# Transposes of an attention kernel on 32-row tiles, four at a time, into the score banks

## The chip, the core and the metric
The kernel runs on one core of one Trainium2 chip. The metric is the device time of one execution in microseconds (us). Before the change it was 661.67 us, the median of 3 runs (661.62 to 662.46). The core has five engines with queues of their own: TensorE (PE; the profile shows its weight loads as PEld), VectorE (DVE), ScalarE (ACT), GpSimd (POOL) and SyncE (SP, which only issues DMAs here).

## The reference
Attention with 12 heads of 32 channels over 64 batch elements of 128 tokens and 384 channels, then a residual and a normalisation without weights. Both encodings are `adj`, so the bias is twice `adj`.

```python
scale = 384 ** (-0.5)
q = (x @ Wq.T).reshape(b, n, 12, 32)
k = (x @ Wk.T).reshape(b, n, 12, 32)
v = (x @ Wv.T + bv).reshape(b, n, 12, 32)
bias = (adj + adj)[:, None]
scores = einsum('bqhd,bkhd->bhqk', q, k) * scale + bias
row_nonzero = any(scores != 0, axis=-1, keepdims=True)
scores = where(row_nonzero, scores, -inf)
p = nan_to_num(softmax(scores, axis=-1))
out = einsum('bhqk,bkhd->bqhd', p, v).reshape(b, n, h)
x = layernorm(x + (out @ Wo.T + bo))
```

## The kernel before
Everything is float32. The four weight products are each made of three matmuls in the rounded form fp32r (high by high, high by low, low by high: `TERMS`), so x, the weights and the attention output are split into a high part (a copy to fp32r on ACT) and a low part (a subtraction on POOL or DVE).

Batch elements are worked on one by one, in an order written out by hand for each engine. Keys and queries are projected for a group of four batch elements together (`GRP`): six tiles (`TILES`) of 128 channels by 512 tokens, three of keys and three of queries, nine matmuls each (`project`, L279). `projected(b)` (L153) deals these six tiles to four iterations as 2, 1, 2, 1, one group ahead of their use. Iteration b then does the following on PE (L375 to L398): scores of b+1 (`score`, L296: per head one product of 32 channels, so the array is used as four tiles of 32 rows, and head j of each four goes to bank `scores_ps[j]`), the transposes of the softmax numerators of b in three turns of four heads (`turn`, L325), the values of b+1 (`values`, L311), the projections in between, the output projection of b-1 (`project_out`, L357), the transposes of the normalising factors (`turn_scale`, L332) and the product of numerators and values (`attend`, L342: 128 rows, 32 columns of weights).

All transposes write one PSUM bank, `pt_ps`, which is emptied each time: four heads by ACT (L466), twice four by DVE (`keep_turned`, L511), the factors by ACT (L481). One bank, `qk_ps`, takes the projections of keys and queries, one, `vo_ps`, both the values and the output projection, and one, `att_ps`, the attention. Four are the score banks.

DVE (L571 to L587) reads the scores, adds the bias and finds the row maxima (`bias_and_max`, L498), adds the value bias (`keep_v`, L507), finds the factors (`find_scale`, L518 to L526), multiplies the attention by them (`normalise`, L534), makes its low part (`attention_low`, L538) and the residual with its statistics (`residual`, L547 to L552). ACT (L459 to L484) has the exponentials with row sums (L409, four heads in `softmax_top`), the copies of projected tiles (`keep`, L420), the high parts of the attention (L431) and of x (`split_x_high`, L426) and the end of the normalisation (L439). POOL (L250 to L258) has the tree that adds up scores to see whether a row is zero (`sum_scores`, L230), the output bias (L219), the inverse deviation (L238 to L244) and the low part of x (`split_x_low`, L212). The split of x for group g runs two groups ahead, in iterations with b % 4 of 0, 1 and 2; the first tile of a group waits for all of it at L273.

Of the kernel before, what the change touches and what calls it, by code (L numbers as in the profile page):

```python
# [10 lines left out]
P = 128  # L11
# [15 lines left out]
TERMS = ((HI, HI), (HI, LO), (LO, HI))  # L27
TREE = 3
# [4 lines left out]
def build(nc, xt, xn, adj, wq, wk, wv, wo, bv, bo, out):  # L33
    with ExitStack() as ctx:
# [27 lines left out]
        probs_t = sb("probs_t", [P, HEADS, P])  # L62
# [5 lines left out]
        scale_t = sb("scale_t", [P, HID])  # L68
# [24 lines left out]
        first_ps = [*scores_ps, qk_ps, vo_ps]  # L93
# [28 lines left out]
        pt_first = sem("pt_first")  # L122
        pt_rest = sem("pt_rest")
# [6 lines left out]
        scale_turned = sem("scale_turned")  # L130
        scale_t_ready = sem("scale_t_ready")
# [71 lines left out]
        def _(pool):  # L203
# [46 lines left out]
            for b in range(-1, NB + 2):  # L250
                if has(b - 2):
                    find_rstd(b - 2)
                if has(b):
                    add_bias(b)
                if has(b + 1):
                    sum_scores(b + 1)
                if 0 <= b and b % GRP < KT and b // GRP + 2 < NG:
                    split_x_low(b // GRP + 2, b % GRP)  # L258

        @block.tensor  # L260
        def _(pe):
            def run_idle(count):

                for _ in range(count):
                    nc.tensor.matmul(pt_ps[:].rearrange("p j q -> p (j q)"), zeros[:, 0:P], zeros[:], start=True,  # L265
                                     stop=True)

            def project(tile):
# [3 lines left out]
                if t == 0:  # L272
                    pe.wait_ge(x_split, KT * g)  # L273
                if tile == 0:
                    pe.wait_ge(first_keys, KT)
                wait(pe, kept, tile)
                for k in range(KT):
                    for n, (a, c) in enumerate(TERMS):
                        last = nc.tensor.matmul(qk_ps[:], w[:, a, k, cols], x_t[:, g % XBUFS, c, k],  # L279
                                                start=(k == 0 and n == 0),  # L280
                                                stop=(k == KT - 1 and n == len(TERMS) - 1))
                last.then_inc(proj_done, 1)
# [45 lines left out]
            def turn_scale(b):  # L328
                pe.wait_ge(scale_ready, b + 1)
                pe.wait_ge(pt_rest, 2 * b + 2)  # L330
                for m in range(KT):
                    last = nc.tensor.transpose(pt_ps[:, m], scale_n[:, b % 2, m * P:(m + 1) * P], ident[:])  # L332
                last.then_inc(scale_turned, 1)

            def attend(b):

# [38 lines left out]
            for b in range(-1, NB + 1):  # L375
                tiles = projected(b)
                if has(b + 1):
                    score(b + 1)
                if has(b):
                    turn(b, 0)  # L380
                if len(tiles) == 2:
                    project(tiles[0])
                if has(b + 1):
                    values(b + 1)
                if has(b):
                    turn(b, 1)
                if tiles:
                    project(tiles[-1])
                if has(b):
                    turn(b, 2)  # L390
                if has(b - 1):
                    project_out(b - 1)
                if has(b):
                    turn_scale(b)
                    attend(b)
                if b == NB - 1:
                    pe.wait_ge(scale_t_ready, NB)
# [3 lines left out]
        def _(act):  # L401
            def softmax_top(b, m):
                act.wait_ge(biased, KT * b + m + 1)
                if m == 0:
                    wait(act, turned, KT * (b - 1))
# [8 lines left out]
            def keep(tile):  # L414
# [5 lines left out]
                nc.scalar.activation(dst[:, g % 2, t % KT], qk_ps[:], ACT.Copy, scale=scale).then_inc(kept, 1)  # L420

            def split_x_high(g, k):
# [3 lines left out]
                nc.scalar.activation(x_t[:, g % XBUFS, HI, k], x_raw[:, g % 2, k], ACT.Copy).then_inc(x_high, 1)  # L426

# [31 lines left out]
            for b in range(-1, NB + 2):  # L459
                tiles = projected(b)  # L460
                if has(b - 1):
                    attention_high(b - 1)
                if has(b):
                    act.wait_ge(turned, KT * b + 1)
                    wait(act, pv_done, b)
                    nc.scalar.activation(probs_t[:, 0:HPT], pt_ps[:], ACT.Copy).then_inc(pt_first, 1)  # L466
                if has(b + 1):
                    softmax_top(b + 1, 0)
                if len(tiles) == 2:
                    keep(tiles[0])  # L470
                if has(b + 1):
                    softmax_top(b + 1, 1)
                    softmax_top(b + 1, 2)
                if tiles:
                    keep(tiles[-1])
                if has(b - 2):
                    normalised(b - 2)
                if has(b):
                    act.wait_ge(scale_turned, b + 1)
# [143 lines left out]
```

## Time and profile before

| | |
|---|---|
| median of 3 runs | 661.67 us |
| the profiled execution | 661.33 us |
| its span, first to last instruction | 659.5 us |
| granted TensorE clock | 0.999 of full speed |
| PE, ACT, DVE, POOL busy | 638.3, 517.6, 502.6, 410.4 us |
| HBM traffic | 68 GB/s over the span |

The span is the profiled execution less some 1.8 us around it. A busy PE is not PE at its peak: matmuls overlap and their ends are modelled, so the distance from one start to the next tells more than one record's duration. Idle time of the other engines costs nothing as long as PE does not wait for them.

### The profile page before, as it was taken

The page shows a single profiled execution, that of the slowest core. Times are in us where ns is not written, and L with a number is a line of the kernel's source. Part 1 is how long each engine was busy: PE and PEld are TensorE (multiplying, and loading weights), DVE is VectorE, ACT ScalarE, POOL GpSimd, SP SyncE. Part 2 cuts the span into 40 slices and gives each one's busy share as a digit, 9 for nine tenths or more (in the row PEclk, how much of TensorE's full clock was granted, in tenths as well). Part 3 has the DMA queues.
Part 4 walks back from the last instruction along what each step waited for, and adds up shares of the span by engine and source line. Part 5 has one row for each costly group of instructions (what it writes and reads, how often), then busy time and mean ns, then how long its engine had stood idle before and what let it go on. Part 6 is the DMA issues. An engine that isn't in the chain of part 4 may idle for free.

```text
span 659.5 us, 18322 instructions
## 1 busy us (share of the span) xinstructions
PE 638.3 (97%) x6060; PEld 550.3 (83%) x6060; DVE 502.6 (76%) x2319; ACT 517.6 (78%) x1942; POOL 410.4 (62%) x500
## 2 busy tenths in 40 slices
PE   9999999999999999999999999999999999999774
PEld 5788888888888888888888888888888888888673
DVE  4667887877887777887877887777877877877884
ACT  5678887878878788877878878788877878877782
POOL 1557665756756666765766856666765756845662
PEclk9999999999999999999999999999999999999999
DMA  9300312121121210212121131210212111011111
GB/s 306 122 4 9 106 57 105 57 74 44 48 105 58 104 50 19 95 59 104 58 86 41 38 106 58 104 50 29 85 58 105 57 50 36 32 58 58 49 49 49
DMA packets 17951, 45.88 MB, mean 70 GB/s; under 512 B 1984, under 2 KB 7104, under 8 KB 17856
## 3 DMA queue, kind: packets, MB, share of 16 engines
q1 hardware_dynamic: 17424, 44.11, 19.3%
q8 instruction: 49, 0.80, 0.5%
q10 hardware_dynamic: 432, 0.59, 0.3%
q14 instruction: 46, 0.38, 0.2%
HBM read 32.11 MB, written 12.58 MB: 68 GB/s over the span
## 4 chain that ended last, share of the span: by engine, by line
PE 67%; POOL 16%; issue 8%; DVE 7%; ACT 2%; POOLq 0%
PE qk_ps L279 21%; PE vo_ps L357 11%; POOL tree L230 10%; PE vo_ps L311 10%; PE pt_ps L325 9%; PE scores_ps L296 6%; PE att_ps L342 5%; DVE nscores L498 4%; POOL x_t L212 4%; PE pt_ps L332 2%; ACT probs L409 2%; PE scores_ps L369 1%; PE pt_ps L265 1%; POOL x_n L219 1%; DVE att_t L538 1%
## 5 line engine op out<-in xcount | busy, mean ns | idle before, releaser
L409 ACT ACTIVATE probs<-nscores,neg_max 128x128 f32<-128x128 f32 x768 | 296.7, 391 | 3.1 <-DVE neg_max L498 3.1
L498 DVE CUSTOM_DVE_ANT_0 nscores<-scores_ps,adj_n 128x128 f32<-128x128 f32 x768 | 171.6, 286 | 16.0 <-PE scores_ps L296 16.0
L409 ACT ACTIVATION_READ_ACCUMULATOR probs<-nscores,neg_max 128x1 f32 x768 | 146.5, 191 | 0.0
L230 POOL TENSOR_TENSOR tree<-nscores 128x768 f32<-128x768 f32 x64 | 120.2, 1878 | 36.0 <-DVE neg_max L498 36.0
L325 PE MATMUL pt_ps<-ident,probs 128*128 128x128 f32 x768 | 118.7, 277 | 9.2 <-ACT probs L409 7.0
L357 PE MATMUL vo_ps<-w_o,att_t 128*128 128x384 f32 x576 | 116.8, 347 | 0.0
L212 POOL TENSOR_TENSOR x_t<-x_raw,x_t 128x512 fp32r<-128x512 f32 x45 | 58.4, 1300 | 93.5 <-ACT x_t L426 93.5
L311 PE MATMUL vo_ps<-w_v,x_t 128*128 128x384 f32 x576 | 114.1, 342 | 0.0
L325 PEld LDWEIGHTS pt_ps<-ident,probs 128*128 128x128 f32 x768 | 89.8, 140 | 28.9 <-ACT probs L409 7.9
L230 POOL TENSOR_TENSOR tree<-tree 128x384 f32<-128x384 f32 (+1 forms) x128 | 103.8, 811 | 10.0
L279 PE MATMUL qk_ps<-x_t,w_k 128*128 128x512 f32 x405 | 105.4, 404 | 2.6 <-POOL x_t L212 2.6
L279 PE MATMUL qk_ps<-x_t,w_q 128*128 128x512 f32 x405 | 105.3, 404 | 0.0
L511 DVE COPY probs_t<-pt_ps 128x512 f32<-128x512 f32 x128 | 87.4, 683 | 19.9 <-PE pt_ps L325 19.9
L311 PEld LDWEIGHTS vo_ps<-w_v,x_t 128*128 128x128 f32 x576 | 100.0, 188 | 2.8
L357 PEld LDWEIGHTS vo_ps<-w_o,att_t 128*128 128x128 f32 x576 | 97.9, 189 | 0.8 <-DVE att_t L538 0.8
L279 PEld LDWEIGHTS qk_ps<-x_t,w_k 128*128 128x128 f32 x405 | 72.7, 188 | 20.1 <-POOL x_t L212 6.0
L279 PEld LDWEIGHTS qk_ps<-x_t,w_q 128*128 128x128 f32 x405 | 72.7, 188 | 14.1
L547 DVE TENSOR_TENSOR y<-vo_ps,x_n 128x384 f32<-128x384 f32 x64 | 35.7, 557 | 53.5 <-PE vo_ps L357 53.5
L219 POOL TENSOR_TENSOR x_n<-x_n,bo_rows 128x384 f32<-128x384 f32 x64 | 65.1, 1017 | 17.4 <-DMA x_n<-xn 17.4
L431 ACT ACTIVATE att_t<-att_ps 128x384 fp32r<-128x384 f32 x64 | 31.4, 491 | 45.3 <-DVE att_ps L534 45.3
L507 DVE TENSOR_TENSOR v_n<-vo_ps,bv_rows 128x384 f32<-128x384 f32 x64 | 35.5, 555 | 40.6 <-PE vo_ps L311 40.6
L481 ACT ACTIVATE scale_t<-pt_ps 128x384 f32<-128x384 f32 x64 | 31.4, 491 | 44.5 <-PE pt_ps L332 43.2
(56 smaller groups left out, 808.2 us busy)
## 6 DMA issues: line engine op xcount, KB each, us to landing
x_n<-xn SPq DMA_DIRECT2D x32, 384.0 KB, 3.6
out<-out_n SPq DMA_DIRECT2D x32, 384.0 KB, 2.6
x_raw<-xt SPq DMA_DIRECT2D x15, 768.0 KB, 5.4
adj_n<-adj SPq DMA_DIRECT2D x32, 128.0 KB, 2.0
x_raw<-xt SPq DMA_DIRECT2D x3, 256.0 KB, 5.5
nscores<-wq ACTq DMA_DIRECT2D x3, 192.0 KB, 4.2
nscores<-wk SPq DMA_DIRECT2D x3, 192.0 KB, 5.5
probs<-wv SPq DMA_DIRECT2D x1, 576.0 KB, 6.4
```

The costliest lines, as they stand in the source:

```text
L212: nc.gpsimd.tensor_tensor(x_t[:, g % XBUFS, LO, k], x_raw[:, g % 2, k], x_t[:, g % XBUFS, HI, k].bitcast(F32), ALU.subtract).then_inc(x_sp ...
L219: nc.gpsimd.tensor_tensor(row, row, bo_rows[:], ALU.add).then_inc(xb_ready, 1)
L230: nc.gpsimd.tensor_tensor(tree[:, b % 2, :, 0:width], src[:, :, 0:width], src[:, :, width:2 * width], ALU.add).then_inc(tree_step, 1)
L279: last = nc.tensor.matmul(qk_ps[:], w[:, a, k, cols], x_t[:, g % XBUFS, c, k], start=(k == 0 and n == 0), stop=(k == KT - 1 and n == len(T ...
L296: last = nc.tensor.matmul(scores_ps[j][:, m * P:(m + 1) * P], q_t[rows, g % 2, m, cols], k_t[rows, g % 2, m, cols], start=True, stop=True)
L311: last = nc.tensor.matmul(vo_ps[:, 0:HID], x_t[:, g % XBUFS, a, k, cols], w_v[:, c, k], start=(k == 0 and n == 0), stop=(k == KT - 1 and n ...
L325: last = nc.tensor.transpose(pt_ps[:, j], probs[:, b % 2, m * HPT + j], ident[:])
L357: last = nc.tensor.matmul(vo_ps[:, 0:HID], att_t[:, a, k], w_o[:, c, k], start=(k == 0 and n == 0), stop=(k == KT - 1 and n == len(TERMS) ...
L409: last = nc.scalar.activation(probs[:, b % 2, h], nscores[:, b % 2, h], ACT.Exp, bias=neg_max[:, b % 2, h:h + 1], scale=-1.0, accum_out=ro ...
L498: last = nc.vector.tensor_tensor_reduce(out=nscores[:, half, h], in0=scores_ps[j][:, m * P:(m + 1) * P], in1=adj_n[:, b // 2 % 2, half], s ...
L511: nc.vector.tensor_copy(probs_t[:, m * HPT:(m + 1) * HPT], pt_ps[:]).then_inc(pt_rest, 1)
L547: nc.vector.tensor_tensor(y[:, half], vo_ps[:, 0:HID], x_n[:, b // 2 % 2, half], ALU.add).then_inc(y_ready, 1)
```

## The change
- The numerators are transposed in pieces of 32 tokens. `turn` takes, for each head, four transposes of 32 rows by 128 keys with a 32x32 piece of the identity, one on each row tile, into the four score banks; then, after a wait for `scale_ready`, the three tiles of factors in the same manner. That is 48 + 12 transposes in place of 12 + 3, in one stretch, after the scores in these banks have been read (`biased`). Each bank ends up with 15 x 32 columns.
- `probs_t` grows by three tiles and takes numerators and factors together (`scale_t` goes). ACT copies two of the banks (`keep_turned_low`), DVE two (`keep_turned_high`); `attend` and `normalise` wait for both.
- `pt_ps` goes, and `qk_ps` gets a second bank, used by turns. The six tiles of a group are dealt as 2, 1, 2, 1, with one before the values and, where there are two, the second after the turn.
- On ACT the first eight heads come before the copies, the last four after; on DVE all heads' biases come first, then `find_scale`, `attention_low`, `keep_v`, the copies and `residual`.
- x is split one iteration sooner (`split_in`), and the first projection waits for its parts one at a time.

```diff
-        qk_ps = ps("qk_ps", [P, 512])
+        qk_ps = [ps(f"qk_ps{i}", [P, 512]) for i in range(2)]
-        pt_ps = ps("pt_ps", [P, HPT, P])
 
         def projected(b):
             if b < -1 or b > NB - GRP - 2:
-                return ()
-            period, s = divmod(b + 1, GRP)
-            first = period * TILES + (0, 2, 3, 5)[s]
-            return tuple(range(first, first + (2, 1, 2, 1)[s]))
+                return (), ()
+            tile = (b + 1) // 2 * 3
+            if b % 2 == 1:
+                return ((tile, 0, FULL),), ((tile + 1, 0, FULL),)
+            return ((tile + 2, 0, FULL),), ()
+
+        def split_in(b):
+            g, k = (b + 1) // GRP + 2, (b + 1) % GRP
+            return ((g, k),) if k < KT and g < NG else ()
+
+        def turned_rows(j):
+            return probs_t[:, :, j * D:(j + 1) * D]
+
+        def turned_bank(j):
+            return scores_ps[j][:, 0:(HEADS + KT) * D].rearrange("p (h q) -> p h q", q=D)
...
-            def turn(b, m):
-                pe.wait_ge(probs_ready, KT * b + m + 1)
-                if m == 0:
-                    wait(pe, scale_t_ready, b)
-                elif m == 1:
-                    pe.wait_ge(pt_first, b + 1)
-                else:
-                    pe.wait_ge(pt_rest, 2 * b + 1)
-                for j in range(HPT):
-                    last = nc.tensor.transpose(pt_ps[:, j], probs[:, b % 2, m * HPT + j], ident[:])
+            def turn(b):
+                pe.wait_ge(probs_ready, KT * (b + 1))
+                pe.wait_ge(biased, KT * (min(b + 1, NB - 1) + 1))
+                for h in range(HEADS):
+                    for j in range(HPT):
+                        rows = slice(j * D, (j + 1) * D)
+                        nc.tensor.transpose(scores_ps[j][:, h * D:(h + 1) * D], probs[rows, b % 2, h],
+                                            ident[rows, rows])
+                pe.wait_ge(scale_ready, b + 1)
+                for m in range(KT):
+                    for j in range(HPT):
+                        rows = slice(j * D, (j + 1) * D)
+                        last = nc.tensor.transpose(scores_ps[j][:, (HEADS + m) * D:(HEADS + m + 1) * D],
+                                                   scale_n[rows, b % 2, m * P:(m + 1) * P], ident[rows, rows])
                 last.then_inc(turned, 1)
...
             for b in range(-1, NB + 1):
-                tiles = projected(b)
+                ahead, behind = projected(b)
                 if has(b + 1):
                     score(b + 1)
-                if has(b):
-                    turn(b, 0)
-                if len(tiles) == 2:
-                    project(tiles[0])
+                for tile, first, end in ahead:
+                    project(tile, first, end)
                 if has(b + 1):
                     values(b + 1)
                 if has(b):
-                    turn(b, 1)
-                if tiles:
-                    project(tiles[-1])
-                if has(b):
-                    turn(b, 2)
+                    turn(b)
+                for tile, first, end in behind:
+                    project(tile, first, end)
                 if has(b - 1):
                     project_out(b - 1)
                 if has(b):
-                    turn_scale(b)
                     attend(b)
...
+            def keep_turned_low(b):
+                act.wait_ge(turned, b + 1)
+                wait(act, pv_done, b)
+                for j in range(2):
+                    nc.scalar.activation(turned_rows(j), turned_bank(j), ACT.Copy).then_inc(turned_low, 1)
...
                 if has(b + 1):
                     softmax_top(b + 1, 0)
+                    softmax_top(b + 1, 1)
+                for tile, _, end in ahead:
+                    if end == FULL:
+                        keep(tile)
+                if has(b):
+                    keep_turned_low(b)
+                for tile, _, end in behind:
+                    if end == FULL:
+                        keep(tile)
                 if has(b + 1):
-                    softmax_top(b + 1, 1)
                     softmax_top(b + 1, 2)
...
-            def keep_turned(b, m):
-                dve.wait_ge(turned, KT * b + m + 1)
-                nc.vector.tensor_copy(probs_t[:, m * HPT:(m + 1) * HPT], pt_ps[:]).then_inc(pt_rest, 1)
+            def keep_turned_high(b):
+                dve.wait_ge(turned, b + 1)
+                wait(dve, pv_done, b)
+                for j in range(2, HPT):
+                    nc.vector.tensor_copy(turned_rows(j), turned_bank(j)).then_inc(turned_high, 1)
...
                 if has(b - 1):
                     normalise(b - 1)
                 if has(b + 1):
-                    bias_and_max(b + 1, 0)
+                    for m in range(KT):
+                        bias_and_max(b + 1, m)
+                if has(b):
+                    find_scale(b)
                 if has(b - 1):
                     attention_low(b - 1)
                 if has(b + 1):
-                    bias_and_max(b + 1, 1)
-                    bias_and_max(b + 1, 2)
                     keep_v(b + 1)
                 if has(b):
-                    keep_turned(b, 1)
-                    find_scale(b)
-                    keep_turned(b, 2)
+                    keep_turned_high(b)
                 if has(b - 1):
                     residual(b - 1)
```

## Rows read from the trace of the kernel before

**Rows 1.** The page, part 1: busy us (share of span) and instructions of each engine.
```profile
PE 638.3 (97%) x6060; PEld 550.3 (83%) x6060; DVE 502.6 (76%) x2319; ACT 517.6 (78%) x1942; POOL 410.4 (62%) x500
```

**Rows 2.** Windows, from scores to scores: three iterations, and one near the end; columns are explained below.
```profile
303.87:312.58 8.71, 8.71 (x95) 7.70 (x91) 7.60 (x37) 7.48 (x30) 5.54 (x7) 1.00 0.44 155
312.58:323.38 10.80, 10.80 (x104) 9.38 (x100) 7.78 (x37) 8.48 (x32) 6.76 (x8) 1.00 0.10 35
...
332.08:343.34 11.26, 11.08 (x103) 9.42 (x99) 7.78 (x37) 8.31 (x31) 6.75 (x8) 1.00 0.10 34
...
616.99:625.58 8.59, 6.84 (x86) 6.06 (x82) 7.60 (x37) 6.79 (x28) 5.50 (x7) 1.00 0.23 79
```

The columns of that answer are the stretch, its length, then the busy time of PE, PEld, DVE, ACT and POOL with the instructions seen, the granted clock, the DMA share and GB/s.

**Rows 3.** Waits: engine, line waited for: us in total, times, longest.
```profile
PE qk_ps L279 <- POOL x_t L212: 2.6, 14, 0.2
```

**Rows 4.** Chain of waits, in order of time: start us, us, what.
```profile
22.12 2.28 PE qk_ps L279 x9
...
301.23 1.58 PE vo_ps L357 x9
...
303.14 0.79 PE att_ps L342 x24
303.94 0.88 PE scores_ps L296 x24
304.81 0.59 PE pt_ps L325 x4
305.40 1.58 PE vo_ps L311 x9
306.98 0.44 PE pt_ps L325 x4
307.42 2.09 PE qk_ps L279 x9
```

**Rows 5.** PEld's timeline round the first turn (start us, us, what); a window of the scores alone.
```profile
304.74 0.42 PEld L325 LDWEIGHTS pt_ps<-ident,probs 128*128 128x128 f32 x4
304.80 0.14 PEld L325 LDWEIGHTS pt_ps<-ident,probs 128*128 128x128 f32 x1
303.86:303.88 0.03, 0.02 (x4) 0.02 (x4) 1.00 0.57 123
```

**Rows 6.** Groups by form: busy us, mean ns | idle before.
```profile
L325 PEld LDWEIGHTS pt_ps<-ident,probs 128*128 128x128 f32 x768 | 89.8, 140 | 28.9 <-ACT probs L409 7.9 <-issue 2.8
...
L296 PEld LDWEIGHTS scores_ps<-k_t,q_t 32*128 32x128 f32 x1536 | 48.6, 186 | 13.9 <-issue 13.9
```

**Rows 7.** DVE's timeline through the same iteration: start us, us, what.
```profile
302.85 0.56 DVE L547 TENSOR_TENSOR y<-vo_ps,x_n 128x384 f32<-128x384 f32 x1 [0.89 <-PE vo_ps L357]
...
304.14 0.55 DVE L534 TENSOR_TENSOR att_ps<-att_ps,scale_t 128x384 f32<-128x384 f32 x1
304.88 0.29 DVE L498 CUSTOM_DVE_ANT_0 nscores<-scores_ps,adj_n 128x128 f32<-128x128 f32 x1 [0.20 <-PE scores_ps L296]
...
305.73 0.55 DVE L538 TENSOR_TENSOR att_t<-att_ps,att_t 128x384 fp32r<-128x384 f32 x1
306.20 0.28 DVE L498 CUSTOM_DVE_ANT_0 nscores<-scores_ps,adj_n 128x128 f32<-128x128 f32 x1
...
307.88 0.55 DVE L507 TENSOR_TENSOR v_n<-vo_ps,bv_rows 128x384 f32<-128x384 f32 x1
308.35 0.68 DVE L511 COPY probs_t<-pt_ps 128x512 f32<-128x512 f32 x1
308.95 0.22 DVE L518 RECIPROCAL recip<-row_sum 128x12 f32<-128x12 f32 x1
...
310.11 0.68 DVE L511 COPY probs_t<-pt_ps 128x512 f32<-128x512 f32 x1
```

**Rows 8.** ACT's timeline, two heads' exponentials in a row.
```profile
325.44 0.39 ACT L409 ACTIVATE probs<-nscores,neg_max 128x128 f32<-128x128 f32 x1
...
325.83 0.39 ACT L409 ACTIVATE probs<-nscores,neg_max 128x128 f32<-128x128 f32 x1
```

More of the change, by code:

```diff
@@ L91, in build @@
         nonzero = att_ps[:, HID + HEADS:HID + 2 * HEADS]
-        first_ps = [*scores_ps, qk_ps, vo_ps]
+        first_ps = [*scores_ps, qk_ps[1], vo_ps]
         x0_in = [sem(f"x0_in{k}") for k in range(KT)]
@@ L256, in _ @@
                     sum_scores(b + 1)
-                if 0 <= b and b % GRP < KT and b // GRP + 2 < NG:
-                    split_x_low(b // GRP + 2, b % GRP)
+                for g, k in split_in(b):
+                    split_x_low(g, k)
         @block.tensor
@@ L264, in run_idle, with project @@
                 for _ in range(count):
-                    nc.tensor.matmul(pt_ps[:].rearrange("p j q -> p (j q)"), zeros[:, 0:P], zeros[:], start=True,
-                                     stop=True)
-            def project(tile):
+                    nc.tensor.matmul(qk_ps[0][:], zeros[:, 0:P], zeros[:], start=True, stop=True)
+            def project(tile, first, end):
                 g, t = tile // TILES + 1, tile % TILES
                 w, cols = (w_k, w_q)[t // KT], slice(t % KT * P, (t % KT + 1) * P)
[L272 to L282, printed above, removed]
+                if first == 0:
+                    wait(pe, kept, tile - 1)
+                    if tile == 1:
+                        pe.wait_ge(first_keys, KT)
+                for i in range(first, end):
+                    k, (a, c) = i // len(TERMS), TERMS[i % len(TERMS)]
+                    if t == 0 and i % len(TERMS) == 0:
+                        pe.wait_ge(x_split, KT * (g - 1) + k + 1)
+                    last = nc.tensor.matmul(qk_ps[tile % 2][:], w[:, a, k, cols], x_t[:, g % XBUFS, c, k],
+                                            start=(i == 0), stop=(i == FULL - 1))
+                if end == FULL:
+                    last.then_inc(proj_done, 1)
             def score(b):
@@ L314, in values @@
                 last.then_inc(vproj_done, 1)
-            def turn(b, m):
-                pe.wait_ge(probs_ready, KT * b + m + 1)
-                if m == 0:
-                    wait(pe, scale_t_ready, b)
-                elif m == 1:
-                    pe.wait_ge(pt_first, b + 1)
-                else:
-                    pe.wait_ge(pt_rest, 2 * b + 1)
-                for j in range(HPT):
-                    last = nc.tensor.transpose(pt_ps[:, j], probs[:, b % 2, m * HPT + j], ident[:])
-                last.then_inc(turned, 1)
[L328 to L333, printed above, removed]
+            def turn(b):
[12 more added lines that the diff above has]
+                                                   scale_n[rows, b % 2, m * P:(m + 1) * P], ident[rows, rows])
+                last.then_inc(turned, 1)
             def attend(b):
+                pe.wait_ge(turned_low, 2 * (b + 1))
+                pe.wait_ge(turned_high, 2 * (b + 1))
                 pe.wait_ge(v_ready, b + 1)
@@ L404, in softmax_top @@
                 if m == 0:
-                    wait(act, turned, KT * (b - 1))
+                    wait(act, turned, b - 1)
                     wait(act, recip_done, b - 1)
@@ L419, in keep @@
                 dst, scale = ((k_t, 1.0), (q_t, 0.5 * SCALE))[t // KT]
-                nc.scalar.activation(dst[:, g % 2, t % KT], qk_ps[:], ACT.Copy, scale=scale).then_inc(kept, 1)
+                nc.scalar.activation(dst[:, g % 2, t % KT], qk_ps[tile % 2][:], ACT.Copy, scale=scale).then_inc(kept, 1)
             def split_x_high(g, k):
@@ L459, in _ @@
             for b in range(-1, NB + 2):
-                tiles = projected(b)
+                ahead, behind = projected(b)
                 if has(b - 1):
                     attention_high(b - 1)
[L463 to L466, printed above, removed]
                 if has(b + 1):
                     softmax_top(b + 1, 0)
-                if len(tiles) == 2:
-                    keep(tiles[0])
+                    softmax_top(b + 1, 1)
[5 more added lines that the diff above has]
+                for tile, _, end in behind:
+                    if end == FULL:
+                        keep(tile)
                 if has(b + 1):
-                    softmax_top(b + 1, 1)
                     softmax_top(b + 1, 2)
-                if tiles:
-                    keep(tiles[-1])
                 if has(b - 2):
                     normalised(b - 2)
-                if has(b):
-                    act.wait_ge(scale_turned, b + 1)
-                    wait(act, att_done, b)
-                    nc.scalar.activation(scale_t[:].rearrange("p (m q) -> p m q", m=KT), pt_ps[:, 0:KT],
-                                         ACT.Copy).then_inc(scale_t_ready, 1)
-                if 0 <= b and b % GRP < KT and b // GRP + 2 < NG:
-                    split_x_high(b // GRP + 2, b % GRP)
+                for g, k in split_in(b):
+                    split_x_high(g, k)
         @block.vector
@@ L524, in find_scale @@
                 dve.wait_ge(nonzero_done, b + 1)
-                wait(dve, scale_turned, b - 1)
+                wait(dve, turned, b - 1)
                 nc.vector.scalar_tensor_tensor(out=scale_n[:, half].rearrange("p (h d) -> p h d", h=HEADS),
```

19 lines of the change are left out of this document (10 added, 9 removed).

## The prediction
> **What bounds the kernel now.** The page comes first. TensorE (PE) is busy 97% of the span, the next engine 78% [rows 1]; so what counts is the order of work on PE and whatever makes it wait. The windows say how even that is: from the start of one iteration's scores to the next, an iteration, which is one batch element, takes 8.71, 10.80, again 8.7 and then 11.26 us, PE busy all through but for the last [rows 2]. The short ones project one tile of keys or queries, the long ones two. The second long one differs from the first by 0.46 us and by nothing that it computes: PE is busy 11.08 of 11.26 us there. The waits name it: 14 times the first projection of a group waits for POOL's split of x [rows 3]. The busy column shows 0.18 us of it; the rest is hidden in modelled ends, and the two lengths of iteration price it better: 0.46 us, 14 times, 6.4 us.
>
> Then the chain of waits through a short iteration, which here is PE alone. One iteration is scores 0.88, first turn 0.59, values 1.58, second turn 0.44, a projection 2.09, third turn 0.44, output projection 1.58, scale turn three quarters of 0.44, attention 0.79: 8.72 us [rows 4]. So 15 transposes of 128x128 cost 0.44/4 = 0.11 each, 1.64 us, and the first of them 0.15 more, because it follows the scores, which use the array as four tiles of 32 rows.
>
> **Part 1, the transposes.** Each 128x128 transpose becomes four of 32 rows, each on its own row tile and into its own bank, moving 32 columns of the identity rather than 128: 60 pairs of weight load and matmul for 15. No row shows this form, so I bound it.
> The matmul's share: 0.11 us is the time of a transpose in a row of them, while its weights load beside it. At a quarter of the columns that is about 0.027 us.
> The weight load's share: it keeps 128 columns. In the first turn the first load starts at 304.74 and the second at 304.80, since nothing is there to overlap the first [rows 5]: 0.06 us. A load of the same width for the scores lasts 186 ns by its record against 140 for a transpose [rows 6], so the transposes' loads are the fast sort, and 0.06 holds for them alone.
> Do four run side by side? The scores are the nearest row: four loads and four matmuls of 32 rows start within a window of 0.025 us [rows 5], and 24 matmuls take 0.88 us, of which 0.19 to 0.22 is switching: six groups at 0.11, so four cost the time of one.
> Value taken: 15 groups of four at the load's 0.061 us, 0.92 us, 0.72 less than now. The ends: 0.027 us a group if only moving counted (0.4 us in all), and 0.112 us a group, what the scores show for a group of four, if a short matmul were no cheaper (1.68 us). The load's width is the same in both forms and cannot shrink, so I take the middle one.
>
> **Part 2, switches between tile shapes.** PE now goes scores, projection, values, turn, output projection, attention. A turn between full-size matmuls is entered and left as a 32-row stage. A projection right after scores took 2.28 us at the start of the kernel against 2.09 elsewhere [rows 4]: 0.19 us to leave the 32-row form. Entering it for the turn costs a drain and an unhidden load; between the 0.15 of the first turn and the 0.22 in the scores' 0.88, with the short load: 0.17. Leaving it again: 0.19. After the scores 0.19 stands where 0.15 stood: 0.04. Going into the attention is the same as now. Sum 0.40 us.
> PE's work per iteration: -0.72 + 0.40 = **-0.32 us**, 8.39 for a short and 10.48 for a long one.
>
> **Part 3, do the others keep up?** The turns are no longer spread out; all heads are turned at once, into the score banks. So a short iteration has a line of waits: scores read out of the banks, turn, copies, attention. I lay it out from the end of an output projection (302.81 in the trace, 301.23 + 1.58), by starts on DVE [rows 7].
> - y starts at +0.04 and normalise at +1.33 (304.14 - 302.81); an operation of 0.55 us lets the next start after 0.47 (v_n at 307.88, copy at 308.35), so the next could start at +1.80. Attention now follows directly and ends on PE at 0.79, the scores at 1.67; DVE can read them 0.06 later. So the biases start at 1.80.
> - Twelve heads: four in 0.85 (304.88 to 305.73), eight in 1.68 (306.20 to 307.88): done at 4.33. PE meanwhile: projection to 3.95 (with 0.19), values to 5.53. The turn's new wait for the biases is met 1.1 us early.
> - find_scale comes before attention_low and keep_v now: 1.16 us (308.95 to 310.11), scale ready at 5.57. PE's heads are turned at 5.53 + 0.17 + 12 x 0.061 = 6.43, so the scale is there, and the turn ends at 6.62.
> - attention_low and keep_v take 0.47 each to the next start; v_n is ready at 5.49 + 0.47 + 0.55 = 6.51. The output projection shares vo_ps and waits for it: it arrives 0.1 us ahead of PE. This is the thin place.
> - Copies: DVE's two of 480 columns, by width of the 512-column one of 0.68, 0.64 each: 6.67 to about 7.9. ACT's two are shorter. PE ends the output projection at 6.62 + 0.19 + 1.58 = 8.39 and needs them then. Hidden by 0.5 us.
> - ACT: heads start 0.39 us apart [rows 8]; eight of them from about 2.8 end at 6.0, a projected tile is kept by 6.6, and it is free for its copies at 6.7. The last four heads come after the copies and must be done one iteration later; ACT is busy 7.5 to 8.5 us of an iteration [rows 2], so that fits with an idle wait of about 1 us before the second tile of a long iteration.
> - A long iteration has 2.09 us more between turn and attention: nothing is late there.
> Total copied is 960 columns on either engine against 896 and 1024: nothing to count.
> What is queued behind the new waits: behind PE's wait for the biases, all PE work; behind its wait for v_n, the output projection and with it y on DVE. As the places are thin, I add 0.1 us for each of 32 short iterations, 3.2 us.
>
> **Part 4, x split one slot sooner.** ACT's high half and POOL's low half (1.28 us) move one iteration ahead, and the DMA that refills x_raw waits for nothing later than now. The wait of the first projection goes with 8 us to spare; next late there is nothing on POOL, busy under 6.8 of each window [rows 2]. -6.4 us.
> The second bank for projections (from pt_ps) removes the wait for `kept` of the tile just before; no row shows that wait, so nothing is gained. The last iterations project nothing and take 8.59 us with PE busy 6.84 [rows 2]: by the layout above the new one is about 8.4. I leave that and the first 28 us at nothing.
>
> **Sum.** 63 x -0.32 = -20.2; -6.4; +3.2: -23.3 us against the profiled execution's 661.3 (span 659.5): 638.0. The median of the runs is 0.3 above the profiled one, inside what runs differ by, so **638.0** stands.
>
> **A rule against this.** In the trace two matmuls on different row tiles start under 0.01 us apart (four in 0.025) [rows 5]. The Trainium skill, "TensorE: Matmul & The Clock Gate", section "Wait — 56ns, not 53.3ns?", says that start-to-start never drops below about 25 ns however few columns move; its Part 3, on packing, has about 4 ns between tiles. By the first, 60 transposes would cost 1.5 us in place of 0.92; by the second nothing changes. The trace sides with the second for 128 columns; with 32 no row tells.
>
> **Rivals.**
> - *Four tiles are no cheaper than one group of the scores* (slower). Place: the turn on PE. Price: 15 x (0.112 - 0.061) = +0.77 us, so +0.45 an iteration, x 63 = +28, less 6.4: about **683**. It decides from a group time of 0.088 us on, where 638 has become 660. For it: the scores are the only 32-row form in the trace and never go below 0.11. Against: their matmuls move 128 columns and come in two passes (24 for 12 heads), and 0.11 is also what 128 moving columns cost a full transpose.
> - *Issue of many short pairs limits it*: a group at about 0.1 us, between the loads' 0.06 and 0.112: +0.27 an iteration, +17 - 6.4, **672**. The skill's 25 ns would be this. Against: the 0.025 us window of four.
> - *Load and move don't overlap on a row tile*: 0.061 + 0.027 = 0.088 a group, +0.08 an iteration: **660**, about no change. Against: at full size 512 columns take 2.09/9 = 0.232 us and 384 take 1.58/9 = 0.176 [rows 4]; at that slope, 0.44 ns a column, 384 columns alone are 0.170, so the load beside them is hidden.
> - *The waits bite*: v_n or the copies come 0.4 us late in each short iteration, as DVE does three things before keep_v: 638 + 31 x 0.3 = **647** beyond the 0.1 allowed. For it: the 0.1 us margin.
>
> **How the numbers follow.** Forecast 0.52, 683: 0.15, 672: 0.10, 660: 0.08, 647: 0.15. The forecast's own range, 630 to 646, has switches that cost half of 0.40 (-12, cut to -8, since DVE's line then binds) and a group at 0.068. The range for 8 in 10 is 630 to 673: it leaves out the 683 and a little below. Faster (by over 0.2%, 1.3 us, about what a measurement of this kernel can tell from no change): 0.52 + 0.15 + half of 0.08 = 0.71; same 0.04; slower 0.25.
>
> **What would show it.** The transposes' 60 records of an iteration in one stretch: 0.9 to 1.1 us right, 1.5 or more the first two rivals. Iterations of 8.4 and 10.5 us. No PE wait for POOL's x_t. PE's idle time before the output projection, with DVE's v_n as releaser, would be the fourth rival. If the iterations alternate at 8.4 and 10.5 but the turn lasts 1.3 us, two errors have cancelled. My forecast fails first if a row-tiled transpose is not loaded at the fast rate.

## The result

The changed kernel takes 642.31 us (median of 4 runs, 642.19 to 642.39) against 661.64: a ratio of 0.9705, 95% interval 0.9688 to 0.9722, 2.9% faster. Forecast were 638.0 us, with 630 to 673 as the range. The profiled execution took 642.19 us, its span is 640.4, 19.1 less than before.

The page, part 1, to be held against [rows 1]:
```profile
PE 620.0 (97%) x8940; PEld 516.5 (81%) x8940; DVE 494.6 (77%) x2319; ACT 518.1 (81%) x1942; POOL 409.5 (64%) x500
```
PE has 2880 more matmuls (60 for 15 in each of 64 turns) and is busy 18.3 us less. DVE, ACT and POOL have as many instructions as they had, and of these only DVE's busy time moves by more than a microsecond (8.0 us less; its two copies have 480 columns and not 512). PE, busy 97% of the span, is still the engine to look at.

Where the 19.1 us lie, in windows from scores to scores of the same batch elements; first before, then after (columns as in [rows 2]):
```profile
36.17:599.71 563.54, 560.92 (x5395) 488.22 (x5392) 438.30 (x2051) 455.89 (x1723) 365.53 (x438) 1.00 0.18 63
599.71:634.15 34.44, 29.18 (x337) 25.84 (x334) 30.41 (x145) 27.65 (x113) 21.92 (x28) 1.00 0.13 45
634.15:659.50 25.35, 15.20 (x146) 11.98 (x142) 14.94 (x54) 10.76 (x35) 9.39 (x17) 0.98 0.16 59
```
```profile
35.99:577.05 541.06, 539.53 (x7960) 453.75 (x7957) 430.35 (x2051) 455.93 (x1726) 364.04 (x438) 1.00 0.20 66
577.05:613.87 36.82, 31.17 (x518) 26.00 (x514) 30.66 (x146) 28.32 (x114) 21.80 (x28) 0.91 0.17 55
613.87:640.40 26.53, 17.05 (x236) 12.97 (x232) 14.86 (x53) 10.85 (x35) 9.43 (x17) 0.82 0.15 52
```
The first line of each is 57 iterations, which give 22.5 us. The last four and the end behind them give back 2.4 + 1.2 = 3.6 us, and there the granted clock (as a share of full speed) is 0.91 and 0.82 where it was 1.00 and 0.98. The first 36 us are 0.2 shorter.

The chain of waits of the changed kernel through one short and one long iteration (the turn is L335 and L341, the projections L291, values L323, output projection L368, attention L353, scores L308), for [rows 4]:
```profile
292.03 0.79 PE att_ps L353 x24
292.82 0.88 PE scores_ps L308 x24
293.70 2.30 PE qk_ps L291 x9
296.00 1.58 PE vo_ps L323 x9
297.58 0.87 PE scores_ps L335 x46
298.45 0.19 PE scores_ps L341 x12
298.64 0.05 issue
298.69 1.81 PE vo_ps L368 x9
...
304.48 1.58 PE vo_ps L323 x9
306.05 0.87 PE scores_ps L335 x48
306.92 0.19 PE scores_ps L341 x12
307.11 2.30 PE qk_ps L291 x9
309.41 1.57 PE vo_ps L368 x9
```
The turn of 60 transposes takes 0.87 + 0.19 = 1.06 us where 15 took 1.64. Three rounds of four take 0.19, so a round takes 0.062 us. A projection takes 2.30 instead of 2.09 after the scores and after the turn: 0.21 us each time PE leaves the 32-row form. An output projection after the turn takes 1.81 for 1.57.

The groups by form, for [rows 6]: the new weight loads last 138 ns, as the old transposes' did (140), and not 186 as the scores' do, and the matmuls move 32 columns.
```profile
L335 PEld LDWEIGHTS scores_ps<-ident,probs 32*128 32x128 f32 x3072 | 53.4, 138 | 20.7 <-issue 15.1 <-ACT probs L414 5.5
L335 PE MATMUL scores_ps<-ident,probs 32*128 32x32 f32 x3072 | 60.3, 224 | 4.4 <-DVE neg_max L504 4.4
```
DVE's timeline through an iteration, from the end of the output projection at 300.50 (298.69 + 1.81), for [rows 7]:
```profile
300.54 0.56 DVE L560 TENSOR_TENSOR y<-vo_ps,x_n 128x384 f32<-128x384 f32 x1 [0.63 <-PE vo_ps L368]
...
301.83 0.57 DVE L545 TENSOR_TENSOR att_ps<-att_ps,probs_t 128x384 f32<-128x384 f32 x1
...
304.83 0.22 DVE L526 RECIPROCAL recip<-row_sum 128x12 f32<-128x12 f32 x1
...
306.00 0.55 DVE L551 TENSOR_TENSOR att_t<-att_ps,att_t 128x384 fp32r<-128x384 f32 x1
306.46 0.55 DVE L513 TENSOR_TENSOR v_n<-vo_ps,bv_rows 128x384 f32<-128x384 f32 x1
307.16 1.22 DVE L519 COPY probs_t<-scores_ps 128x480 f32<-128x480 f32 x2 [0.15 <-PE scores_ps L341]
```
`find_scale` starts at +4.33 (304.83) and v_n is ready at +6.51 (306.46 + 0.55), where the layout put them.

### The profile page after: what moved, and what is told of

Read it like the earlier page. It is cut to its first block, busy times and chain, and to the rows that moved or that the text cites. A ratio compares the mean times of both kernels' runs of the same rounds, so it can differ in the third digit from the quotient of the medians.

```text
span 640.4 us, 24017 instructions
## 1 busy us (share of the span) xinstructions
PE 620.0 (97%) x8940; PEld 516.5 (81%) x8940; DVE 494.6 (77%) x2319; ACT 518.1 (81%) x1942; POOL 409.5 (64%) x500
## 4 chain that ended last, share of the span: by engine, by line
PE 92%; DVE 5%; ACT 1%; issue 1%; POOL 0%; POOLq 0%; DVEq 0%
PE qk_ps L291 32%; PE vo_ps L368 17%; PE vo_ps L323 14%; PE scores_ps L308 8%; PE att_ps L353 8%; PE scores_ps L335 8%; DVE nscores L504 2%; PE scores_ps L341 2%; PE qk_ps L277 1%; PE scores_ps L380 1%; ACT probs L414 1%; DVE att_t L551 1%; DVE v_n L513 0%; DVE stats L563 0%; DVE y L560 0%
## 5 line engine op out<-in xcount | busy, mean ns | idle before, releaser
L504 DVE CUSTOM_DVE_ANT_0 nscores<-scores_ps,adj_n 128x128 f32<-128x128 f32 x768 | 166.8, 286 | 4.7 <-PE scores_ps L308 4.7
L368 PE MATMUL vo_ps<-w_o,att_t 128*128 128x384 f32 x576 | 116.9, 348 | 4.2 <-DVE v_n L513 2.8
L323 PE MATMUL vo_ps<-w_v,x_t 128*128 128x384 f32 x576 | 111.8, 338 | 0.0
L368 PEld LDWEIGHTS vo_ps<-w_o,att_t 128*128 128x128 f32 x576 | 101.8, 192 | 10.2 <-DVE att_t L551 3.4
L323 PEld LDWEIGHTS vo_ps<-w_v,x_t 128*128 128x128 f32 x576 | 102.3, 188 | 6.1
L291 PE MATMUL qk_ps<-x_t,w_q 128*128 128x512 f32 x405 | 106.7, 407 | 0.0
L291 PE MATMUL qk_ps<-x_t,w_k 128*128 128x512 f32 x405 | 106.6, 407 | 0.0
L291 PEld LDWEIGHTS qk_ps<-x_t,w_k 128*128 128x128 f32 x405 | 72.5, 188 | 18.7
L291 PEld LDWEIGHTS qk_ps<-x_t,w_q 128*128 128x128 f32 x405 | 72.5, 188 | 18.7
L519 DVE COPY probs_t<-scores_ps 128x480 f32<-128x480 f32 x128 | 78.1, 652 | 9.2 <-PE scores_ps L341 7.3
L437 ACT ACTIVATE probs_t<-scores_ps 128x480 f32<-128x480 f32 x128 | 66.1, 569 | 14.6 <-PE scores_ps L341 14.0
L335 PEld LDWEIGHTS scores_ps<-ident,probs 32*128 32x128 f32 x3072 | 53.4, 138 | 20.7 <-issue 15.1
L335 PE MATMUL scores_ps<-ident,probs 32*128 32x32 f32 x3072 | 60.3, 224 | 4.4 <-DVE neg_max L504 4.4
L504 DVE DVE_READ_ACCUMULATOR2_ANT neg_max<- 128x1 f32 x768 | 64.0, 83 | 0.0
L308 PE MATMUL scores_ps<-k_t,q_t 32*128 32x128 f32 x1536 | 60.8, 287 | 0.9 <-DVE q_t L581 0.9
```

What stands on the lines that cost most here:

```text
L291: last = nc.tensor.matmul(qk_ps[tile % 2][:], w[:, a, k, cols], x_t[:, g % XBUFS, c, k], start=(i == 0), stop=(i == FULL - 1))
L308: last = nc.tensor.matmul(scores_ps[j][:, m * P:(m + 1) * P], q_t[rows, g % 2, m, cols], k_t[rows, g % 2, m, cols], start=True, stop=True)
L323: last = nc.tensor.matmul(vo_ps[:, 0:HID], x_t[:, g % XBUFS, a, k, cols], w_v[:, c, k], start=(k == 0 and n == 0), stop=(k == KT - 1 and n ...
L335: nc.tensor.transpose(scores_ps[j][:, h * D:(h + 1) * D], probs[rows, b % 2, h], ident[rows, rows])
L368: last = nc.tensor.matmul(vo_ps[:, 0:HID], att_t[:, a, k], w_o[:, c, k], start=(k == 0 and n == 0), stop=(k == KT - 1 and n == len(TERMS) ...
L437: nc.scalar.activation(turned_rows(j), turned_bank(j), ACT.Copy).then_inc(turned_low, 1)
```

## The experiments

Each was run beside the kernel before on the same chip. The median of that kernel was 661.6 us there, and 660.9 on the chip that ran experiments 3, 4, the second filler and the full-size transposes at the end. So a comparison of times from two chips is open by up to 0.8 us.

**1. The form of the transposes alone.** The new order and banks, but with full-size transposes.
```diff
-                for h in range(HEADS):
-                    for j in range(HPT):
-                        rows = slice(j * D, (j + 1) * D)
-                        nc.tensor.transpose(scores_ps[j][:, h * D:(h + 1) * D], probs[rows, b % 2, h],
-                                            ident[rows, rows])
+                for m in range(KT):
+                    for j in range(HPT):
+                        nc.tensor.transpose(scores_ps[j][:, m * P:(m + 1) * P], probs[:, b % 2, m * HPT + j], ident[:])
```
(The scale's three are full-size likewise, and the copies follow the layout.)

> The changed kernel with its transposes at full size again: 12 of 128x128 for the heads and 3 for the scale, still all in one stretch and into the four score banks, the same queues otherwise. If the gain of the iteration comes from the 32-row form: PE pays 15 x 0.109 = 1.64 us in place of 1.06 for the turn and 0.22 for leaving the 32-row form, so +0.36 us in each of 62 iterations, +22: about 664.5 us. If it comes from the new order and the banks (turning all heads in one stretch, copies of both engines together), the form makes little difference and the time stays within 642 to 646 us.

Measured: 657.60 us, ratio 0.9939 (0.9924 to 0.9954). The chain, a long and then a short iteration:
```profile
296.39 1.31 PE scores_ps L334 x12
297.70 0.33 PE scores_ps L337 x3
298.03 2.10 PE qk_ps L291 x9
...
307.25 1.31 PE scores_ps L334 x12
308.56 0.33 PE scores_ps L337 x3
308.88 1.58 PE vo_ps L363 x9
```
The turn is 1.64 us again and nothing is paid behind it. Iterations take 8.76 and 10.86 us, +0.29 and +0.39 over the changed kernel, on average close to the 0.36 expected; over the same 57 iterations that is 19.2 us (560.21 for 541.06). Yet the whole is only 15.3 us longer and not 22. The rest is in the last iterations: the last three take 8.47 to 8.48 here, at full clock, and 8.47, 10.00 and 9.88 in the changed kernel, and the end behind them takes 24.9 us here and 26.5 there. This was the first sign that the short form costs something at the end. Against the kernel before, this version is 4 us faster: that is what the order and the early split give together, 6.4 us for the split less some 3 us (0.05 an iteration), since PE now goes from the scores into a projection and not into a transpose. So of the 19.3 us of the change some 15 are the form's, net of what it loses at the end, and 4 the rest's.

**2. The split of x, both ways round.** In the changed kernel back to its old slot, and in the kernel before one slot sooner.
```diff
-            g, k = (b + 1) // GRP + 2, (b + 1) % GRP
-            return ((g, k),) if k < KT and g < NG else ()
+            g, k = b // GRP + 2, b % GRP
+            return ((g, k),) if b >= 0 and k < KT and g < NG else ()
```


> The changed kernel with x split in the old slot. If the wait of the first projection for POOL's low half was a term of its own, it comes back 14 times: POOL would end its part about 3.4 us into the iteration, PE wants the third part at about 3.1, so 0.3 to 0.5 us each, 4 to 7 in all: 646 to 649 us. If waiting part by part was already enough to hide it: 642.3 us.

```diff
-                if 0 <= b and b % GRP < KT and b // GRP + 2 < NG:
-                    split_x_low(b // GRP + 2, b % GRP)
+                if (b + 1) % GRP < KT and (b + 1) // GRP + 2 < NG:
+                    split_x_low((b + 1) // GRP + 2, (b + 1) % GRP)
```
(and `split_x_high` on ACT likewise)

> The kernel before with one thing changed, x split one iteration sooner. If the 0.46 us by which every second long iteration is longer is this wait and nothing else: 14 x 0.46 = 6.4 us less, 655.2 us, and all long iterations 10.80. If the wait is only passed on (ACT's or POOL's work in the earlier slot delays another step): over 659 us.

Measured: 648.88 us (646.75 to 650.39), 6.6 over the changed kernel; and 655.19 us, 6.4 under the kernel before (ratio 0.9904, 0.9889 to 0.9919). In the first, the wait is back in the waits:
```profile
PEld qk_ps L291 <- POOL x_t L224: 6.5, 14, 0.6
```
and every second long iteration takes 10.75 in place of 10.47, 3.9 us in 14, just under the 4 to 7 expected. The rest of the 6.6 is not in these iterations. The profiled execution is one of 646.75 us; it has one more iteration of 12.0 us for 10.5, with a granted clock of 0.86, and an end that is shorter than the changed kernel's. The other three executions took 648.8 to 650.4 us at a mean granted clock of 0.984 to 0.986, against 0.989 in the profiled one. So 3.9 us is what this experiment shows of the wait itself. In the second all long ones take 10.80 and the wait is gone from PE's list. So the early split was worth 6.4 us in the kernel before, as the comparison of two iteration lengths had said; the busy column of [rows 3] alone would have given 2.6.

**3. What sets the time of a group of four.** Half the weights, the same 32 moving columns: half of the numerators are left out.
```diff
-                        nc.tensor.transpose(scores_ps[j][:, h * D:(h + 1) * D], probs[rows, b % 2, h],
+                        nc.tensor.transpose(scores_ps[j][0:64, h * D:(h + 1) * D], probs[rows, b % 2, h, 0:64],
```


> The changed kernel transposing only the first 64 of 128 keys of each head (half the numerators are left out, so the weight loads have 64 columns and the matmuls still move 32). If a group of four costs the time of its weight load: 12 groups at about 0.035 in place of 0.062 us, -0.3 us in a long iteration and, since DVE's v_n is met, at most -0.1 in a short one: 630 to 634 us. If the moving or the issue of pairs sets the group's time: the turn keeps its 0.87 us and the time stays at 642.

Measured: 634.36 us (one of four runs 629.5, the others 634.2 to 634.8). PE's timeline of a short iteration:
```profile
293.00 0.59 PE L335 MATMUL scores_ps<-ident,probs 32*64 32x32 f32 x48
293.42 0.35 PE L341 MATMUL scores_ps<-ident,scale_n 32*128 32x32 f32 x12
294.17 1.12 PE L368 MATMUL vo_ps<-w_o,att_t 128*128 128x384 f32 x5 [0.40 <-DVE v_n L513]
```
48 transposes now start within 0.42 us (293.00 to 293.42), not 0.76: 0.035 us a round. So the weight columns set the time, not the 32 moved ones, and the issue of pairs does not limit it down to 0.009 us each. That it is the load itself is argued: the edit also halves the partitions that each transpose writes. Long iterations fall from 10.47 to 10.12. Short ones stay at 8.47: what PE saves it waits, for v_n. That DVE's line ends them, by a hair, in the changed kernel too is shown in experiment 6. The 57 iterations save 10.4 us, but the whole saves only 8.0, a little less than the 8 to 12 expected: the last four take 38.1 us at a granted clock of 0.87, where the changed kernel needed 36.8 at 0.91.

**4. Side by side or not.** The same 48 transposes, one row tile after the other.
```diff
-                for h in range(HEADS):
-                    for j in range(HPT):
+                for j in range(HPT):
+                    for h in range(HEADS):
```


> The changed kernel with the two loops of the heads' turn exchanged: all twelve heads on one row tile, then the next. The work is the same. If the gain is that four row tiles load and move side by side: 48 loads of 0.061 us one after another, 2.9 us in place of 0.73, +2.2 us an iteration, about 780 us. If weight loads overlap in whatever order they come: 642 us.

Measured: 780.5 us (two runs, 777 and 784). The number is the one expected, by two errors that cancel. Two short iterations, from scores to scores, one at full clock and one not:
```profile
148.14:158.09 9.95, 9.95 (x140) 8.67 (x136) 7.56 (x37) 7.62 (x30) 6.74 (x8) 1.00 0.28 94
309.61:321.08 11.47, 11.47 (x140) 9.98 (x136) 7.82 (x37) 8.84 (x32) 6.92 (x9) 0.85 0.44 150
```
And the turn of the second of them on PE, with the clock of that stretch and of one behind it:
```profile
314.37 2.33 PE L335 MATMUL scores_ps<-ident,probs 32*128 32x32 f32 x45
314.40:316.85 2.45, 2.45 (x61) 2.45 (x60) 1.00 (x3) 0.93 (x4) 2.45 (x2) 1.00 0.60 227
318.00:320.00 2.00, 2.00 (x7) 1.59 (x5) 0.33 (x1) 2.00 (x10) 0.74 (x2) 0.50 0.00 0
```
At full clock a short iteration is 9.95 us long, +1.5 and not +2.2: 48 transposes on one row tile at a time take 0.05 us each. That is some 95 of the 138 us over 63 iterations; the rest goes with the clock, granted at 0.917 over the span. In the second iteration the clock is at full speed through the turn and at half behind it, and PE's records have no gap in either iteration. That the order of tiles decides holds; 0.062 us buys four transposes in one order and little more than one in the other. The 0.05 also says that loading one row tile and moving through it fit into less than the 0.062 us of a round, so a round is not exactly one load; what its last 0.01 us are is open.

**5. The last iterations.** In the changed kernel the last of them run like this on PE:
```profile
594.87 1.85 PE L323 MATMUL vo_ps<-w_v,x_t 128*128 128x384 f32 x9
597.83 0.94 PE L335 MATMUL scores_ps<-ident,probs 32*128 32x32 f32 x48 [1.11 <-DVE neg_max L504]
598.90 0.38 PE L341 MATMUL scores_ps<-ident,scale_n 32*128 32x32 f32 x12
599.92 2.89 PE L368 MATMUL vo_ps<-w_o,att_t 128*128 128x384 f32 x9 [0.64 <-DVE v_n L513]
602.74 1.32 PE L353 MATMUL att_ps<-probs_t,v_n 128*32 128x128 f32 x24
```
PE waits 1.11 and 0.64 us for DVE, which costs nothing by itself, as the iteration would be 8.47. But then the output projection takes 2.89 us for nine matmuls where it took 1.81, and the attention 1.32 for 0.86: together the 1.5 us by which this iteration is longer. The granted clock is at half speed there:
```profile
600.50:603.50 3.00, 3.00 (x24) 2.51 (x26) 1.02 (x3) 1.99 (x9) 1.99 (x3) 0.50 0.00 0
```
Three kernels fill or replace something in the last five iterations.

One idle matmul (512 columns of zeros into a free bank, `run_idle`) before the turn:
```diff
+                if has(b) and not ahead:
+                    run_idle(1)
                 if has(b):
                     turn(b)
```


> The changed kernel with one idle matmul pair (512 columns of zeros into a free projection bank, about 0.9 us) before the turn in the last five iterations, where PE waits 1.1 us for DVE. If the 3.5 us that the last iterations cost more than before are the granted clock falling to half while PE has gaps: the clock stays at 1.00 to near the end, and the time is 639 to 640 us. If the clock is not what lengthens them (or the gap before the output projection alone makes it fall): 642 us or more.

A second one of 256 columns behind the turn:
```diff
+                if has(b) and not ahead:
+                    run_idle(1, 256)
                 for tile, first, end in behind:
```


> The changed kernel with both of PE's gaps in the last five iterations filled, one idle matmul of zeros of 512 columns before the turn and one of 256 before the output projection. The first alone did not keep the clock up. If the second gap (0.64 us) was what was left: clock 1.00, 638 to 639.5 us. If matmuls of zeros of this kind don't keep it up at all: two stretches at half clock as before, 641 to 643 us.

Full-size transposes there, the short ones elsewhere:
```diff
-                for h in range(HEADS):
+                full = b >= NB - GRP - 1
+                if full:
+                    for m in range(KT):
+                        for j in range(HPT):
+                            nc.tensor.transpose(scores_ps[j][:, m * P:(m + 1) * P], probs[:, b % 2, m * HPT + j],
+                                                ident[:])
+                for h in range(0 if full else HEADS):
```
(the scale and the copies' layout likewise)


> The changed kernel, but with full-size transposes (15 of 128x128) in its last five iterations, where PE waits for DVE anyway. In the kernel with full-size transposes throughout, the granted clock stayed at 1.00 there and three iterations took 8.47 to 8.48 us; in the changed kernel the clock halves in stretches and two of them take 10.0 and 9.9. If the clock follows from how little the short transposes work the array: 8.47 for all of them, and the end shorter by 1 to 1.6 us, about 638 us, a version faster than both. If it follows from PE's gaps as the records show them (about the same in both kernels): no change, 642 us.

Measured: 641.18, 638.51 (637.49 to 639.29) and 639.31 us (638.82 to 639.83). Windows of one of the last iterations, in this order:
```profile
594.10:604.08 9.98, 8.95 (x132) 7.17 (x128) 7.72 (x37) 6.86 (x29) 5.41 (x7) 0.83 0.24 82
```
```profile
594.24:602.71 8.47, 8.07 (x135) 6.18 (x131) 7.46 (x37) 6.85 (x29) 5.22 (x7) 1.00 0.29 97
```
```profile
595.44:603.90 8.46, 7.08 (x85) 6.02 (x81) 7.41 (x37) 6.88 (x29) 4.86 (x6) 1.00 0.29 97
```
One filler doesn't keep the clock, and the expectation for it was wrong: two of its last iterations still take 9.98 and 9.95 us, and the whole falls only from 642.3 to 641.2. Two fillers keep it, and so do full-size transposes with no filler at all, though their PE is busy 7.08 us and the one with a filler 8.95 of 9.98. So the busy time that the records show doesn't tell whether the clock holds.

Is it the gaps? In the changed kernel they are 1.11 and 0.64 us, with one filler 0.26 and 0.64, with full-size transposes 1.12 and 0.26: the version with one filler has less idle time than the one with full-size transposes, and loses the clock. The kernel before has a single gap of 1.76 us in such an iteration and keeps it:
```profile
613.74 0.63 PE L325 MATMUL pt_ps<-ident,probs 128*128 128x128 f32 x4 [1.76 <-ACT probs L409]
```
And experiment 4 loses it without a gap. From the start of the values to the output projection 5.1 us pass both in the changed kernel (586.40 to 591.45) and with full-size transposes (587.84 to 592.90); what differs in them is the form of the transposes and how long they take (1.06 and 1.64 us). So the gaps alone don't decide. Nor is the 32-row form alone enough, as most iterations with it run at 1.00, or needed: with full-size transposes throughout, the end behind the last scores has 0.92. In the last iterations it makes the difference; what about it does was not separated.

**6. DVE's line, and both together.** `TREE = 4` for `TREE = 3`: POOL adds once more, DVE's sum reads 8 columns a head.

> The changed kernel itself, on the chip of the next three, as their base: 642 us, short iterations 8.47, long ones 10.47.

> The changed kernel with a fourth step of POOL's tree (about 0.4 us more on POOL), so that DVE's sum in find_scale reads 8 columns a head and not 16, about 0.1 us less. If DVE's line from the scores to v_n is what ends the short iterations: they go from 8.47 to PE's own 8.41 at most, long ones stay, 1.5 to 2 us less in all, 640.3. If PE's own work ends them: 8.47, 642. If POOL's extra step makes the sum late: above 643.

> The kernel with both gaps of the last iterations filled, again, beside the changed kernel on the same chip: 3 to 4 us less than it.

> Both: the two add, 4.5 to 6 us less than the changed kernel, about 637 us, if one works in the short iterations and the other in the last five alone.

Measured, on one chip: 642.43, 639.83, 637.97 and 635.87 us. Short iterations go to 8.37 to 8.39 with the fourth step, long ones stay at 10.47, and in the chain PE no longer waits before the output projection:
```profile
297.25 0.19 PE scores_ps L341 x12
297.44 1.78 PE vo_ps L368 x9
299.22 0.79 PE att_ps L353 x24
```
The gain is 2.6 us where at most 2 was expected; the short iterations fall by 0.09 us, so DVE's line did end them. The two edits nearly add: their parts give 2.6 + 4.5 = 7.1 us, measured are 6.6, a little over the 4.5 to 6 expected. The version with both is faster than either kernel: ratio 0.9612 (0.9598 to 0.9625) to the kernel before, against 0.9708 (0.9692 to 0.9723) for the changed one there.

## Why the prediction was nearly right

- **The transposes** (0.92 for 1.64 us forecast): right, mechanism and size. In the changed kernel a group of four costs 0.062 us: 48 take 0.87, 0.12 of it to enter the form. The value came from two starts of weight loads in one turn, 0.06 us apart [rows 5], and experiment 3 shows that the weight columns set it. Some of the exact match is luck: experiment 4 has load and move of one row tile in 0.05 us, so the 0.061 was not the load alone. The rivals at 0.112 and 0.1 us a group are out. Why the scores need 0.11 was not tested: their matmuls move 128 columns, and their loads last 186 ns by the records.
- **The rule of the Trainium skill** ("TensorE: Matmul & The Clock Gate", section "Wait — 56ns, not 53.3ns?") that start-to-start never falls below about 25 ns: by it the turn would take 1.5 us. It takes 1.06, switch included, and experiment 3 reaches 0.009 us a transpose. For matmuls on different row tiles the measurement decides against it; its Part 3, with about 4 ns between tiles, is not contradicted.
- **The switches** (0.40 us): right in the sum. 0.12 to enter (0.17 forecast), 0.21 to leave (0.19), and 0.06 more after the scores (0.04).
- **Load and move on one row tile in series**: not what happens. A group would take 0.088 us, and one of 64 weight columns, by half the load, some 0.058; they take 0.062 and 0.035.
- **The layout of the waits**: right to 0.02 us on DVE, and its thin place is the one that was named: v_n before the output projection. The allowance of 0.1 us for each short iteration covers what is there: 8.47 against PE's own 8.37 to 8.41. The rival that this place costs 0.4 us fell.
- **The early split** (-6.4 us): right, shown alone in the kernel before (6.4). In the changed kernel the iterations show 3.9 us of it; that waiting part by part hides the rest is likely but was not run alone.
- Together, for the 57 iterations in the windows above, the steps give 57 x 0.32 + 6.4 - 28 x 0.1 = 21.8 us; measured 22.5.
- **The term that failed: "I leave that and the first 28 us at nothing."** For the last iterations I looked at the waits alone, found that DVE ends them either way, and priced them at zero or a little below. They cost 3.6 us more. What was cheaper on PE there came in iterations where PE waits already, and the granted clock fell to half for stretches of them. Experiments 1 and 5 show it from both sides: full-size transposes at the end, or fillers in both gaps, bring back 8.47 us an iteration, and 3.0 us of the whole (full-size transposes, times from two chips) to 4.5 us (two fillers, on one chip).
- **The sum** doesn't keep to that sentence: it takes 0.32 us in all 63 iterations, six of them outside the 57, and so books some 1.5 us of gain where the text leaves nothing. Outside the 57 the forecast has 1.5 us gained and the runs 3.4 lost; inside, the runs gain 0.7 more than forecast. That is the 4.3 us between forecast and result, 0.1 for rounding.

What stays open is which work keeps the clock; the runs tell it apart only as in experiment 5. Nor was it looked into why some profiled executions (the late split, full-size transposes at the end, two fillers in their second run, the fillers with the fourth step) have a stretch of lower clock between 36 and 40 us too, in an iteration of 11.6 to 12.0 us in place of 10.5. The changed kernel's own profile has none there.

## What to carry to other kernels

Small transposes and products on separate row tiles pay if they are issued round the tiles, not tile by tile, and then cost about the time of one weight load per round; count also about 0.2 us each time PE leaves the form. Price a wait by two lengths of an iteration that differ in nothing else, not by the idle column. And when PE gets faster work where it waits anyway, look at the clock there: a stage that is free by the waits can lose its clock.

## What the runs showed of the hardware

Issued round the row tiles, four 32-row transposes with 128 weight columns and 32 moved ones take 0.062 us, and 0.035 with 64 weight columns. Issued one row tile after the other, each takes 0.05 us. Entering that form cost 0.12 us here and leaving it for full-size matmuls 0.21.

The granted clock fell from 2.4 to 1.2 GHz in stretches where PE's records are dense (experiment 4: PE busy in all of 11.47 us, the clock 1.00 through the turn and 0.50 from 318 to 320 us), so dense records are no promise of a full clock. In the changed kernel it was 0.50 from 600.5 to 603.5 us, behind a turn, and nine matmuls of 384 columns took 2.89 us for 1.81.
